# Chaining the last layer of a six-layer decoder kernel into the program of the two layers ahead of it

## What is computed

```python
x = _layernorm(x + _L1_attn_ref(x, ...))       # relative attention
x = _layernorm(x + _L1_xattn_ref(x, ctx, ctx, ...))   # mLSTM
x = _layernorm(x + _L1_ffn_ref(x, ...))        # product keys
...
# _L1_ffn_ref
q = jnp.einsum('bnd,de->bne', x, w_q)
mean = jnp.mean(q, axis=(0, 1))
var = jnp.var(q, axis=(0, 1))
q = (q - mean) * jax.lax.rsqrt(var + BN_EPS) * bn_gamma + bn_beta
sim = jnp.einsum('pbnhd,hkpd->pbnhk', q.reshape(...), keys)
...
h = gelu_new(jnp.einsum('bnd,bnhkd->bnhk', x, down_embed[indices]))
out = jnp.einsum('bnhk,bnhkd->bnd', softmax(scores) * h, up_embed[indices])
```

## Time and profile before

| | us |
|---|---|
| median of three runs | 1852.7 |
| lowest, highest | 1849.7, 1853.59 |
| the profiled execution, its time | 1848.75 |
| its span, first to last instruction | 1847.0 |
| TensorE busy in it | 1627.0 (88%) |
| VectorE busy | 1205.2 (65%) |
| ScalarE busy | 675.7 (37%) |
| GpSimd busy | 270.4 (15%) |

### The profile page before, as it was taken

The page is one execution under the profiler, slowest core; times in us unless marked ns, Lnnn a source line. Parts: engine busy times, 40 slices in busy tenths (PEclk is TensorE's granted clock), DMA queues, the critical chain, the costliest instruction groups (busy, mean ns, idle before and its releaser), DMA issues. The chain is left out here.

```text
span 1847.0 us, 38518 instructions
## 1 busy us (share of the span) xinstructions
PE 1627.0 (88%) x14744; PEld 1276.6 (69%) x14744; DVE 1205.2 (65%) x3876; ACT 675.7 (37%) x1409; POOL 270.4 (15%) x241
## 2 busy tenths in 40 slices
PE   6899987889988678888888879498899999999998
PEld 4677765656656556777776658376788788878876
DVE  4555653455555635566666548538889889889884
ACT  3333331255555246556666433013222222222210
POOL 1444444100000100000000015201001001000100
PEclk9899998999999879999999965699999999999999
DMA  3100000000011369989998710440000000000000
GB/s 124 46 18 18 18 24 6 18 19 25 25 59 41 105 240 319 320 316 320 323 326 317 234 44 26 167 203 1 2 7 7 13 2 14 13 2 13 2 7 13
DMA packets 96469, 175.32 MB, mean 95 GB/s; under 512 B 16032, under 2 KB 80800, under 8 KB 91552
## 3 DMA queue, kind: packets, MB, share of 16 engines
q1 hardware_dynamic: 96288, 172.85, 27.0%
HBM read 93.01 MB, written 79.69 MB: 94 GB/s over the span
## 5 line engine op out<-in xcount | busy, mean ns | idle before, releaser
L104 PE MATMUL bank<-per_xT,per_down 128*128 128x256 f32 x1024 | 250.6, 390 | 2.3 <-ACT per_xT L2540 1.6
L2843 PE MATMUL bank<-per_up,per_act_w 128*128 128x256 f32 x1024 | 242.3, 382 | 0.0
L2843 PEld LDWEIGHTS bank<-per_up,per_act_w 128*128 128x128 f32 x1024 | 195.4, 192 | 27.0
L104 PEld LDWEIGHTS bank<-per_xT,per_down 128*128 128x128 f32 x1024 | 190.3, 192 | 29.9 <-issue 2.7
L2547 ACT ACTIVATE per_act_w<-bank 128x512 f32<-128x512 f32 x128 | 76.2, 597 | 364.2 <-PE bank L104 329.6
L1503 ACT ACTIVATE rel_probs<-later_shared,rel_low 128x256 f32<-128x256 f32 x256 | 117.2, 518 | 26.9 <-DVE rel_low L1587 26.8
L1587 DVE CUSTOM_DVE_ANT_0 later_shared<-bank,later_shared 128x256 f32<-128x256 f32 x256 | 95.0, 420 | 36.9 <-PE bank L1701 19.2
L920 DVE TENSOR_REDUCE xat_mx<-bank 128x2 f32<-128x512 f32 x128 | 79.4, 684 | 33.7 <-PE bank L968 33.6
L104 PE MATMUL bank<-ret_x2T,ret_w_in 128*128 128x256 f32 x384 | 93.0, 399 | 7.5 <-issue 7.5
L1722 PE MATMUL bank<-rel_band_k,later_shared 32*128 32x191 f32 x512 | 63.9, 368 | 32.2 <-DVE rel_low L1587 24.5
L2526 POOL TENSOR_TENSOR per_sim<-per_sim,per_best_i 128x512 f32<-128x512 f32 x32 | 41.9, 1329 | 332.9 <-DVE per_sim L2660 332.9
(11 more groups left out here) (359 smaller groups left out, 3187.3 us busy)
## 6 DMA issues: line engine op xcount, KB each, us to landing
rel_qr_rows<-later_shared SPq DMA_DIRECT2D x32, 1024.0 KB, 8.5
rel_p_rows<-rel_probs SPq DMA_DIRECT2D x32, 1024.0 KB, 6.9
later_shared<-rel_qr_rows SPq DMA_DIRECT2D x64, 384.0 KB, 4.5
rel_by_dist<-rel_p_rows SPq DMA_DIRECT2D x64, 384.0 KB, 4.7
per_down<-in_per_down SPq DMA_DIRECT2D x1, 4096.0 KB, 25.0
per_up<-in_per_up SPq DMA_DIRECT2D x1, 4096.0 KB, 13.6
ret_xin<-in_x SPq DMA_DIRECT2D x8, 256.0 KB, 2.9
xat_cT<-in_contextT SPq DMA_DIRECT2D x8, 256.0 KB, 3.0
```

The costliest lines, as they stand in the source:

```text
L104: last = pe.matmul(dst, wt[:, c], src[:, c, :], start=c == 0, stop=c == DC - 1)
L2843: last = pe.matmul(tiles(bank[7])[:, t, :], act_w[:, n % 2, k, t * P:t * P + P], up[:, k, :], start=k == 0, stop=k == COLS - 1)
```

## The change

The last layer becomes a third set of generators in the block of `later_layers`. Its early buffers are allocated on the other side of the memory, its steps are taken by `beside` in the mLSTM's steps, and x comes from the mLSTM's tile `mls_yout`. The number of semaphores is reduced by merging.

```diff
@@ mlstm_layer
-    x_loaded, c_loaded = [sem(f"x_loaded{b}") for b in range(nb)], [sem(f"c_loaded{b}") for b in range(nb)]
-    v_loaded = [sem(f"v_loaded{b}") for b in range(nb)]
+    x_loaded = [sem(f"x_loaded{k}") for k in range(3)]
+    c_loaded, v_loaded = sem("c_loaded"), sem("v_loaded")
...
-            pe.wait_ge(c_loaded[b], 16)
+                pe.wait_ge(c_loaded, 16 * nb)
...
-            pe.wait_ge(v_loaded[b], 16 * TT)
-            pe.wait_ge(v_ones, 1)
+            if U == 0:
+                pe.wait_ge(v_loaded, 16 * TT * nb)
+                pe.wait_ge(v_ones, 1)
...
+            beside(s)
...
+    def give_x(sp, b, to, done):
+        sp.wait_ge(stored[b % 2], 16 * (b // 2 + 1))
+        sp.dma_start(to, batch_of(x_out, b)).then_inc(done, 16)
+    def result(engine, b):
+        engine.wait_ge(y_ready, b + 1)
+        return yout[:, b % 2]
+    def finished(engine):
+        for k in range(2):
+            engine.wait_ge(stored[k], 16 * (nb // 2))
@@ peer_layer, SyncE
+        for s in BESIDE:
+            if s == 0:
+                load_all(sp, loaded, [(wq, w["wq"]), (wqT, w["wqT"]), (cols[:], w["cols"])])
+                sp.dma_start(keys, w["keys"]).then_inc(keys_loaded, 16)
+            if s in (10, 12, 14):
+                m = s // 2 - 5
+                before["give_x"](sp, m, xin[:, m], x_read[m])
+            yield
+        before["finished"](sp)
         sp.dma_start(down[:], w["down"]).then_inc(down_loaded, 16)
@@ VectorE
+            if s == 7:
+                dve.wait_ge(centre_mm, 1)
+                for c in range(DC):
+                    last = dve.tensor_scalar(centre[:, c * P:c * P + P], bank[6 + c][:, 3 * P:4 * P], 1.0 / SEQ, None,
+                                             ALU.mult)
+                last.then_inc(centre_ready, 1)
+            if s >= 8 and s % 2 == 0:
+                for n in ((0, 1) if s == 8 else (s // 2 - 3,)):
+                    dve.tensor_tensor(xc[:, n, :, 0:D], before["result"](dve, n),
+                                      centre[:].unsqueeze(1).broadcast_to([P, TT, D]), ALU.subtract).then_inc(xc_ready, 1)
+            if s == 9:
+                dve.wait_ge(loaded, 16 * 3)
+                dve.tensor_copy(beta_wide, over(beta, P)).then_inc(beta_ready, 1)
+            yield
+        before["finished"](dve)
         dve.wait_ge(cov_mm, 1)
@@ TensorE
+            if s == 7:
+                pe.wait_ge(cleared, 1)
+                x = before["result"](pe, 0)
+                for c in range(DC):
+                    for t in range(TT):
+                        last = pe.matmul(bank[6 + c][:, 3 * P:4 * P], ones[:], x[:, t, c * P:c * P + P], ...)
+                last.then_inc(centre_mm, 1)
+                pe.wait_ge(centre_ready, 1)
+            yield
+        before["decays_made"](pe)
         for n in range(nb):
             pe.wait_ge(xc_ready, n + 1)
             ...
+            if n == nb - 2:
+                before["outputs_read"](pe)
+                pe.wait_ge(beta_ready, 1)
+                pe.wait_ge(keys_loaded, 16)
+                ...
+                done.then_inc(bias_mm, 1)
```

More of the change, by code:

```diff
@@ L2330, in chained @@
         for _ in steps:
+            pass
+        for _ in last:
             pass
@@ L2859, in _ @@
-            for b in range(PH):
-                spread(b)
-            pe.wait_ge(beta_ready, 1)
-            pe.wait_ge(keys_loaded, 16)
-            for b in range(BLOCKS):
-                last = pe.matmul(bank[(7, 0)[b // per_bank]][:, b % per_bank * NK:b % per_bank * NK + NK],
-                                 beta_wide[:, b], keys[:, b], start=True, stop=True)
-            last.then_inc(bias_mm, 1)
-            for b in range(PH, BLOCKS):
-                spread(b)
-            weigh_keys(0)
@@ new lines, in weights @@
+        def weights(g):
+            pe.wait_ge(hot_ready, g + 1)
+            if g >= 1:
+                pe.wait_ge(weighted, 2 * g)
+            slot = g % NSLOT
+            for s in range(CH // 2):
+                for k in range(2):
+                    for par in range(2):
+                        own = slice(PICKS * par, PICKS * par + PICKS)
+                        last = pe.matmul(bank[5 + par][:, s * COLS:s * COLS + COLS], hot_x[own, slot, s],
+                                         hot_y[own, slot, k, s], start=k == 0, stop=k == 1)
+            last.then_inc(weights_mm, 1)
@@ new lines, in go_up @@
+        def go_up(n, t, part):
+            if part == 0:
+                pe.wait_ge(weighted, SLOTS * n + PARTS * (t + 1))
+            if t + part == 0:
+                if n == 0:
+                    pe.wait_ge(up_loaded, 16)
+                else:
+                    pe.wait_ge(x_used, n)
+            for k in range(part * COLS // PARTS, (part + 1) * COLS // PARTS):
+                last = pe.matmul(tiles(bank[7])[:, t, :], act_w[n % 2][:, k, t * P:t * P + P], up[:, k, :],
+                                 start=k == 0, stop=k == COLS - 1)
+            last.then_inc(up_mm, 1)
@@ new lines, in tensor @@
+        for b in range(PH):
+            spread(b)
+        for b in range(PH, BLOCKS):
+            spread(b)
+        weigh_keys(0)
+        turn_x(-SLOTS, 0)
+        go_down(0)
+        weigh_keys(1)
+        go_down(1)
+        similar(0)
+        for G in SLOT_RANGE:
+            if (g := weights_of(G)) is not None:
+                weights(g)
+            if (d := down_of(G)) is not None:
+                go_down(d)
+            if (todo := up_of(G)) is not None:
+                go_up(*todo)
+            if (T := tile_at(G, PARTS)) is not None:
+                turn_picks(G, T)
+            if (m := turn_of(G)) is not None:
+                turn_x(G, m)
+            if (T := tile_at(G + 1, 0)) is not None and T >= 1:
+                similar(T)
```

779 lines of the change are left out of this document (372 added, 407 removed).

## The result

The changed kernel takes **1837.0 us** (median of 6 runs, 1833.2 to 1843.9) against 1852.0 (6 runs, 1848.4 to 1853.6) measured beside it: ratio 0.9917, 95% interval 0.9902 to 0.9933. The forecast was 1836.8. The profiled execution took 1833.68 us with a span of 1831.6.

What follows compares the result with a forecast made beforehand. The prediction took TensorE to bound the mLSTM's loop, VectorE a hair behind, with TensorE idle at the hand-over. 22.0 - 7.35 + 1.2 = 15.85 us off the median of 1852.7 gave 1836.8 us, range 1831.5 to 1845.5.

Steps and rivals of the forecast that it cites:

- Terms 1 and 2: Last y to the end of the sums of products: 26.05 us removed, 4.05 us put in its place.
- the slower rival: Products behind the loop and maybe first scores: clock stays at 1.2 GHz, kernel takes 1862 to 1877 us; chance 0.05.
- Term 3: mLSTM loop, ahead of the last y: inserted column sums, copy and subtractions add 7.35 us.
- step 7: mLSTM loop: column sums and TensorE's wait for the centre's copy cost 2.4 us, bounds 2.0 and 3.5.
- steps 8 and 9: mLSTM loop: two subtractions cost 1.3 us, then the copy of beta 1.0 us of its 1.23.
- the single ones: mLSTM loop, steps 10, 12 and 14: one subtraction each, 0.65 us apiece, 1.95 together.
- Step 18: mLSTM loop's tail: batch 6's subtraction, between its y and the last statistics, costs 0.7 us.
- Term 4: Prelude behind the sums: spreads take 16.4 us without the bias, 1.2 us gained, bounds 0 and 2.
- Edits at nothing: Down table's later place, early weights and merged semaphores cost nothing; the table's load goes out near 1187.3.
- the dear loop: mLSTM loop: each insertion costs double, 13.55 us in all, gain 9.65, median 1843 us; chance 0.13.
- the hiding one: mLSTM loop: insertions hide and cost 2.7 to 4 us, gain 19 to 20.5, median near 1833; chance 0.12.
- given back later: Last layer's loop: some 12 of the 16 us gained return, time near 1849.5 us; chance 0.06.

Runs made afterwards that it cites:

- r1_again: The changed kernel run again unchanged, beside three follow-ups: 1837.33 us, ratio 0.9915 to the kernel before.
- r0_again: The changed kernel run once more unchanged: 1835.99 us, ratio 0.9913 to the kernel before.
- e2_reload: Changed kernel, but x is loaded back from memory and all eight subtractions come after the last y: 1849.39 us, ratio 0.9989 to before.
- b_again: The kernel before the change, run again unchanged for a second trace: 1852.20 us, ratio 1.0012.
- e3: Changed kernel with TensorE's wait for the centre moved from the end of step 7 to that step's outputs: 1834.14 us, ratio 0.9909 to before.
- e6: Changed kernel with the subtraction of batch 6 moved from step 18 to behind the last statistics: 1833.70 us, ratio 0.9919 to before.
- e1: Changed kernel without the centre's subtraction for batches 0 to 4, TensorE's products kept (computes something else): 1830.09 us, ratio 0.9883 to before.
- e5: Changed kernel with the bias products moved from behind batch 6 to behind batch 5: 1834.51 us, ratio 0.9889 to before.
- e7: Changed kernel with four unread 128x256 products added in the pauses behind the sums of products: 1836.13 us, ratio 0.9907 to before.
- e8: Changed kernel with eleven unread 128x256 products added ahead of the mLSTM's loop: 1833.84 us, ratio 0.9907 to before.
- e4: Changed kernel with the bias products moved from between batches 6 and 7 to behind the tenth spread: 1833.79 us, ratio 0.9917 to before.
- f5: Changed kernel with the edits of e3, e4 and e7 together: 1831.95 us, ratio 0.9894 to before.

## Why the prediction was right

**Terms 1 and 2**, 22.0 us net, came out at 21.5 (26.05 less 4.58). The pieces of term 2 were further off than their sum: batch 6 was centred 1.80 us behind its y, not 0.75, and batch 7's products ended 9.17 behind it, not 7.85. But the last y came 4.59 behind y of batch 6, not 3.8, and so most of that cancels. The products started right behind the last outputs, at 1166.86 (forecast 1168). The first 48 records ended at 1179.98 (forecast 1180). The clock, against the earlier trace rows:

```profile
1168.00:1172.00 4.00, 4.00 (x11) 3.15 (x10) 3.61 (x10) 0.00 (x0) 2.25 (x2) 0.51 0.20 66
1172.00:1176.00 4.00, 4.00 (x20) 3.50 (x19) 3.53 (x10) 0.63 (x1) 0.97 (x1) 1.00 0.02 4
1192.00:1196.00 4.00, 4.00 (x12) 3.23 (x11) 0.87 (x4) 0.00 (x0) 0.00 (x0) 0.57 0.95 410
```

It rose 5 us after the products began. In eleven traces with the products in this place the rise came 2.3 to 5 us after, and the pause before batch 6 took it up, as the forecast said: 0.94 in this one, 2.2 in r1_again. So the slower rival, in which the clock stays at 1.2 GHz, falls.

**Term 3**, 7.35, came out at 6.6 (r0_again, r1_again). Every insertion was near its price: step 7 2.2 (2.4), steps 8 and 9 1.20 and 1.08 (1.3 and 1.0), the single ones 0.6 each (0.65), step 16 nothing. Step 18 cost 0.2 to 0.4 rather than 0.7. The last two gaps together are 14.52, against 14.21 and 14.34 in the traces of before and 14.08 in e2_reload, which has no subtraction there. Two reasons were off, though. I took TensorE for the loop's bound, with VectorE a hair behind the earlier trace rows; b_again shows the period to be VectorE's, with its wait for GpSimd, at either clock. This left the size alone, since the insertions stand outside that wait and were priced as VectorE's time: step 12's gap is 10.97 in r0_again at a clock of 0.50 and 10.96 in the first trace of after at 0.81. And in step 7 the column sums don't cost their issue; the turn-taking around the centre costs the time (e3). That 1.85 + 0.5 came near 2.23 is luck: the reason was another, and at a full clock the step costs 1.5.

I also wrote that nothing inserted would overlap GpSimd. In steps 8 to 16 that held, with 0.68 and 0.69 us for a subtraction. In step 18 the subtraction ran beside the addition and took 1.77. The 2.92 of the earlier trace rows for the normalisations ahead of it was not the rule of the kernel before. The same place in b_again:

```profile
1176.67 1.68 DVE L141 TENSOR_SCALAR mls_yout<-mls_y,mls_mv,mls_rs 128x256 f32<-128x256 f32 x2
1179.63 0.75 DVE L131 BATCH_NORM_STATS2 mls_st<-mls_y 128x6 f32<-128x256 f32 x2 [1.29 <-POOL mls_y L2040]
```

There, as at this place in every trace but the first, they took 1.68 or 1.69, and VectorE then waited for the addition, 1.29 us where nothing stood between. The new subtraction stands in that wait, and by e2 it costs 0.4 here. The rule that I weighed, of the Trainium skill, GPSIMD Engine Reference, section 1, Specifications, on contention with VectorE instructions that have two SBUF inputs, agrees with the subtraction's 1.77.

**Term 4**, 1.2 gained, is right when the clock holds: 16.29 us for the spreads (r0, e3, e6), forecast 16.4. In seven of the ten traces that have the bias products ahead of the spreads (after, r1, e1, e2, e5, e7, e8) it fell after a pause of 1.70 or 2.10 us, and in one of them, e5, at both. What decides it in an execution is open. Each fall costs 1.65 to 1.7 and takes the whole term back. Where the bias products fill the second pause the clock held there in all four traces (before, b_again, e4, f5), against five of the ten without; that they hold it is likely, not shown. This is the one step that failed in most executions: I counted the pause of 2 to 3 us in the spreads as time lost and not as a place where the clock may fall.

**Edits at nothing** held: the down table is out at 1185.86 (forecast 1187.3) and lands 12.4 us later. **Sum**: 15.85 forecast between the turn and the rest. The three traces of after gave 17.0, 16.0 and 14.3, and the medians 15.0. The span forecast of 1831.1 against 1831.6 is closer than it deserves, since 2.4 us more ahead of the turn and the early clock in the loop (2.7) cancel. So is the median, 1836.8 against 1837.0: it was counted from a before of 1852.7, and the before measured beside it was 1852.0. Of the rivals, the dear loop (13.55) and the hiding one (4.0 and less) both fall with the 6.6 of r0_again and the price that e1 found, and "given back later" with the constant rest.

## What to carry over

Work that waits for a chain's last step should be split so that all but its last part stands ahead of that step, even if feeding it costs the chain's busiest engine its full price: here 6.6 us were paid for 21.5. When two engines in a loop are both nearly full, look for a trace at another clock to see which of them sets the period, and look in the fuller one for small instructions that take several times their length: they may be waiting for a third. When one of two crossed waits is removed, compute what the other then costs. Put work that is free to move into pauses between dense groups of matmuls: it takes itself off the path (the sums end 1.8 us earlier in e4 and e5), and may help to hold the clock.

## What the runs showed of the hardware

- The clock of a loop of small matmuls is not a property of the kernel: from the turn on, the kernel before had 0.50 for 110 us in one execution and 0.83 for 20 us of them in another, with loops of 102.89 and 102.95 us.
- The clock may fall, to near 0.5 for 3 to 4 us, after pauses as short as 1.70 us (with another of 0.59 ahead of it) and 2.10 us behind dense work, in some executions and not in others of the same program.
- A subtraction of 128x512 with both inputs in SBUF takes 0.69 us alone and 1.77 beside a GpSimd addition of 1.26. GpSimd suffers too: its `mls_rs` of 0.71 took 1.08 in e6 beside such a subtraction.
- A small VectorE instruction (128x8, 0.17 us alone) that stands beside a GpSimd instruction on 128x512 is held until 0.02 to 0.03 us behind its end, 92 times behind the addition. The profile counts that as VectorE's busy time.
- The same 4 MB load landed 25.0 us after its issue before and 12.4 after, with 4.6 MB of weights and the loads of x gone from in front of it.
